# Mixing stage of a two-layer kernel: outputs made one step later, masks last in GpSimd's step, and two small jobs that change engines

## The reference, cut to what matters

```
bc = einsum('bti,oi->bto', value, W_bc)          # per token: 32 heads x (Bz, Bx, Cz, Cx) x 32
bc = bc / (sqrt(sum(bc*bc, -1)) + EPS)
step: z = S*(z - dt*A*s + dt*(Bz x u));  s = s + dt*z + dt*(Bx x u)
      y = Cz.z + Cx.s
y = (y + skip*value) * silu(gate)
out = einsum('bti,oi->bto', y, W_out)
```

## Time and profile before

| | us |
|---|---|
| median of 3 runs (1324.44 to 1331.52) | 1328.13 |
| the profiled execution's own time | 1331.72 |
| its span | 1329.6 |
| TensorE busy, share of the span | 96% |
| VectorE busy | 68% |
| ScalarE busy | 49% |
| GpSimd busy | 44% |

### The profile page before, as it was taken

One profiled execution on the slowest core, in us unless ns is written; L12 is line 12 of the kernel. 1 busy time (PEld: TensorE's weight loads), 2 busy tenths in 40 slices (PEclk: granted clock), 3 DMA queues, 4 the chain that ended last, 5 costly groups with the idle time before them and its releaser, 6 DMA issues. The chain is left out here.

```text
span 1329.6 us, 23001 instructions
## 1 busy us (share of the span) xinstructions
PE 1279.4 (96%) x7802; PEld 705.5 (53%) x7802; DVE 910.6 (68%) x1771; ACT 651.5 (49%) x1564; POOL 588.8 (44%) x939
## 2 busy tenths in 40 slices
PE   7999998999999999998899998999999999999999
PEld 4443334566566566565445454555655556544545
DVE  6999996999999999997301206888787786630100
ACT  3265533566665665664322315665565666531221
POOL 2633323888888988987100002444444453500000
PEclk7989999999999999998899999999999999999999
DMA  3369897656656665664100002000000000000000
GB/s 99 127 264 394 338 393 273 215 191 224 201 201 212 220 203 196 223 213 167 64 0 0 1 0 90 1 1 1 1 1 1 2 1 1 1 0 0 16 0 16
DMA packets 72834, 151.38 MB, mean 114 GB/s; under 512 B 7312, under 2 KB 24336, under 8 KB 69904
## 3 DMA queue, kind: packets, MB, share of 16 engines
q1 hardware_dynamic: 66096, 133.66, 28.5%
q10 hardware_dynamic: 6624, 16.26, 3.2%
HBM read 98.78 MB, written 51.12 MB: 113 GB/s over the span
## 5 line engine op out<-in xcount | busy, mean ns | idle before, releaser
L1869 POOL TENSOR_SCALAR pr<-pr,rs,sg 128x512 f32<-128x512 f32 (+3 forms) x256 | 152.6, 614 | 204.9 <-DVE rs L1774 186.1
L720 PE MATMUL banks<-w_bc,valueT 128*128 128x512 f32 x392 | 185.1, 596 | 3.4 <-ACT ent L593 2.4
L1046 DVE TENSOR_TENSOR pp<-banks,ring 128x1024 f32<-128x1024 f32 x128 | 156.1, 1220 | 12.8 <-DVEq L1083 5.5
L1675 ACT ACTIVATE pr<-banks,nm 128x512 f32<-128x512 f32 (+3 forms) x256 | 132.8, 524 | 20.4 <-DVE nm L1768 17.7
L1663 ACT COPY prT<-banks 128x512 f32<-128x512 f32 (+3 forms) x128 | 54.3, 424 | 112.5 <-PE banks L1544 112.3
L1768 DVE TENSOR_REDUCE nm<-banks 128x2 f32<-128x1024 f32 (+3 forms) x128 | 105.5, 824 | 4.4
L1384 DVE TENSOR_TENSOR x<-x,banks 128x256 f32<-128x256 f32 x16 | 6.7, 421 | 148.3 <-PE banks L1295 148.3
L935 ACT COPY qk<-banks 128x512 f32<-128x512 f32 x128 | 74.8, 585 | 63.0 <-PE banks L834 63.0
L672 POOL TENSOR_TENSOR C<-abL,A 128x128 f32<-128x128 f32 x128 | 53.3, 424 | 104.9 <-DVE banks L347 91.8
L1544 PE MATMUL banks<-ident,pr 128*128 128x128 f32 x640 | 96.9, 281 | 2.1 <-POOL pr L1869 0.7
L1130 POOL TENSOR_SCALAR_AFFINE_SELECT bp<-bp 128x1024 f32<-128x1024 f32 x64 | 73.8, 1152 | 55.9 <-ACT bp L942 55.9
(11 more groups left out here) (254 smaller groups left out, 2499.6 us busy)
## 6 DMA issues: line engine op xcount, KB each, us to landing
ring<-psi SPq DMA_DIRECT2D x126, 512.0 KB, 4.4
psi<-ring SPq DMA_DIRECT2D x10, 2048.0 KB, 7.5
psi<-X SPq DMA_DIRECT2D x5, 2048.0 KB, 7.5
det<-w_bc ACTq DMA_DIRECT2D x16, 512.0 KB, 4.7
ring<-det SPq DMA_DIRECT2D x64, 128.0 KB, 4.7
bcs<-ent ACTq DMA_DIRECT2D x30, 256.0 KB, 6.9
ring<-bcs SPq DMA_DIRECT2D x30, 256.0 KB, 5.0
w_bc<-in_w_bc SPq DMA_DIRECT2D x4, 1024.0 KB, 10.9
```

The costliest lines, as they stand in the source:

```text
L720: mm = pe.matmul(bank, m["valueT"][:, c, t * P:(t + 1) * P], w, start=(c == 0), stop=(c == 1))
L1046: dve.tensor_tensor(pp[:, q % 2].rearrange("p (a c) n -> p a c n", c=2), sc.unsqueeze(2).broadcast_to([P, 4, 2, HN]), rec[:, n % RL, q % 2 ...
L1675: act.activation(pr[:, n % RP, h, 0:w], S[n % 2][:, h, 0:w], ACT.Exp, bias=nm[:, n % 4, h:h + 1], accum_out=sm[:, m % 3, n % 2, h:h + 1]). ...
L1869: pool.tensor_scalar(row, row, rs[:, n // 2 % 2, n % 2, h:h + 1], sg[:, TPB * b + it, hd:hd + 1], ALU.mult, ALU.mult).then_inc(s["scaled"], 1)
```

## The change

What is done:

- On TensorE `outputs` of pair p-1 are made in step p, right behind `scores` of pair p. The loop gets one step more. `turn_state` and `project_out` come one step later, in even steps, behind the first `project`, and write into columns 192 to 447 of the bank YG and not into TP. Their waits on other banks go with them.
- On ScalarE `take` moves ahead of the two `copy_qk`, the spreading of the state and the copy to oc stand between them, and `expand_u` is made here for tiles 2 to 15.
- On VectorE `evacuate` is gone. GpSimd makes it, in odd steps.
- On GpSimd both `combine` come first, then `evacuate`, then `mask(p)`, then the rest. `expand_u` stays there for tiles 0 and 1 only.
- The ring ct is three units deep and not two.

The pieces of the diff stand in the order TensorE, ScalarE, VectorE, GpSimd.

```diff
-    RL, RB, RC, RQ = 3, 3, 2, 4
+    RL, RB, RC, RQ = 3, 3, 3, 4
+    STATE = 2 * N + P
...
             def turn_state(t, f):
-                pe.transpose(TP[:, 0:P], hT[:, f].rearrange("p a n -> p (a n)"), k.ident[:]).then_inc(s["turned"], 1)
+                pe.transpose(YG[:, STATE:STATE + P], hT[:, f].rearrange("p a n -> p (a n)"), k.ident[:]).then_inc(s["turned"], 1)
             def project_out(t):
-                    mm = pe.matmul(TP[:, P:2 * P], yg[:, t % 2, f], w_out[:, f], start=(f == 0), stop=(f == 1))
+                    mm = pe.matmul(YG[:, STATE + P:STATE + 2 * P], yg[:, t % 2, f], w_out[:, f], start=(f == 0), stop=(f == 1))
...
-            for p in range(2 - LEAD, PAIRS + 2):
+            for p in range(2 - LEAD, PAIRS + 3):
                 if 0 <= p < PAIRS:
                     scores(2 * p)
                     scores(2 * p + 1)
+                if 1 <= p <= PAIRS:
+                    outputs(2 * p - 2)
+                    outputs(2 * p - 1)
                 for u in range(2):
                     if 0 <= p + 1 < PAIRS:
                         turn_both(2 * p + 2 + u)
                     if 2 <= p + LEAD < PAIRS:
                         project(2 * (p + LEAD) + u)
-                if 0 <= p < PAIRS:
-                    outputs(2 * p)
-                if p >= 3 and p % 2 == 1:
-                    t, f, j = split(2 * (p - 2))
-                    pe.wait_ge(s["qk"], min(2 * p + 4, UNITS))
-                    if passes_on(t):
-                        turn_state(t, f)
-                    if f == 1:
-                        project_out(t)
-                if 0 <= p < PAIRS:
-                    outputs(2 * p + 1)
+                    if p >= 4 and p % 2 == 0 and u == 0:
+                        t, f, j = split(2 * (p - 4))
+                        pe.wait_ge(s["ygc"], min(p, PAIRS) // 2)
+                        if passes_on(t):
+                            turn_state(t, f)
+                        if f == 1:
+                            project_out(t)
...
+                if 2 <= p <= PAIRS and p % 2 == 0:
+                    take(p // 2 - 1)
                 if 0 <= p + 1 < PAIRS:
                     copy_qk(2 * p + 2)
-                    copy_qk(2 * p + 3)
-                if 2 <= p + LEAD < PAIRS:
-                    square(p + LEAD)
-                if p >= 3 and p % 2 == 1:
-                    t, f, j = split(2 * (p - 2))
+                if p >= 4 and p % 2 == 0:
+                    t, f, j = split(2 * (p - 4))
...
+                if 0 <= p + 1 < PAIRS:
+                    copy_qk(2 * p + 3)
+                if 2 <= p + LEAD < PAIRS:
+                    square(p + LEAD)
+                if p >= 4 and p % 4 == 1 and p // 4 + 1 < TILES:
+                    expand_u(p // 4 + 1)
...
                     if passes_on(t):
                         state(t, f)
-                    evacuate(t, f)
...
+            def evacuate(t, f):
+                tok = slice(t * P, (t + 1) * P)
+                pool.wait_ge(s["ygc"], 2 * t + f + 1)
+                if t >= 2:
+                    pool.wait_ge(s["out"], t - 1)
+                pool.tensor_tensor(yg[:, t % 2, f], ygc[:, f, 2 * N:], m["gateT"][:, f, tok], ALU.mult).then_inc(s["yg_done"], 1)
...
                 if p + 1 < PAIRS:
                     combine(2 * p + 3)
+                if p + 2 < PAIRS:
+                    combine(2 * p + 4)
+                if p >= 3 and p % 2 == 1:
+                    t, f, j = split(2 * (p - 2))
+                    evacuate(t, f)
                 if p >= 0:
                     mask(p)
-                if p + 2 < PAIRS:
-                    combine(2 * p + 4)
                 if p >= 7 and p % 4 == 3:
                     residual(p // 4 - 1)
-                if p >= 4 and p % 4 == 1 and p // 4 + 1 < TILES:
-                    expand_u(p // 4 + 1)
```

More of the change, by code:

```diff
@@ L823, in turn_both @@
                     pe.wait_ge(s["qk"], q)
-                if q >= 10 and q % 4 == 2:
-                    t, f, j = split(q - 7)
-                    if passes_on(t):
-                        pe.wait_ge(s["hz"], 2 * (links(t, f) + 1))
-                    if f == 1:
-                        pe.wait_ge(s["oc"], t + 1)
                 for pair in range(2):
@@ L855, in outputs @@
                         pe.wait_ge(s["ygc"], q // 4)
-                    if carried(t):
-                        pe.wait_ge(s["hz"], 2 * (links(t - 1, f) + 1))
+                    if q >= 8:
+                        ts, fs, js = split(q - 8)
+                        if passes_on(ts):
+                            pe.wait_ge(s["hz"], 2 * (links(ts, fs) + 1))
+                        if fs == 1:
+                            pe.wait_ge(s["oc"], ts + 1)
                 for i in range(4):
@@ L963, in spread_state, with expand_u @@
                     act.copy(dst, src).then_inc(s["hz"], 1)
+            def expand_u(t):
+                act.wait_ge(s["yg"], HG * (t - 1))
+                for f in range(2):
+                    dst = uz[:, t % 2, f].rearrange("p (j e) -> p j e", e=DIAG)[:, :, 0:P].rearrange(
+                        "p j (i e) -> p j i e", i=4)[:, :, :, 0:DH]
+                    act.copy(dst, m["u"][:, t, f * P:(f + 1) * P].rearrange("p (i j d) -> p j i d", i=4, j=4)
+                             ).then_inc(s["uz"], 1)
             def moments(t):
@@ L998, in _ @@
                             act.wait_ge(s["x"], t)
-                        act.copy(oc[:], TP[:, P:2 * P]).then_inc(s["oc"], 1)
-                if 0 <= p < PAIRS and p % 2 == 1:
-                    take(p // 2)
+                        act.copy(oc[:], YG[:, STATE + P:STATE + 2 * P]).then_inc(s["oc"], 1)
+                if 0 <= p + 1 < PAIRS:
[4 more added lines that the diff above has]
+                    expand_u(p // 4 + 1)
                 b, i = divmod(p - 20, 16)
@@ L1067, in state @@
                                   tv[:, :, 1].unsqueeze(1).broadcast_to([P, 2, 2, N]), ALU.add).then_inc(s["hT"], 1)
[L1069 to L1074, removed]
             def invert(b):
@@ L1099, in _ @@
                         state(t, f)
-                    evacuate(t, f)
                 if q % 2 == 0 and q // 2 % 16 == 12 and q // 2 >= 28:
                     invert(q // 32 - 1)
-            evacuate(TILES - 1, 0)
-            evacuate(TILES - 1, 1)
         @block.gpsimd
@@ L1160, in _ @@
                     combine(2 * p + 3)
+                if p + 2 < PAIRS:
[3 more added lines that the diff above has]
+                    evacuate(t, f)
                 if p >= 0:
                     mask(p)
-                if p + 2 < PAIRS:
-                    combine(2 * p + 4)
                 if p >= 7 and p % 4 == 3:
                     residual(p // 4 - 1)
-                if p >= 4 and p % 4 == 1 and p // 4 + 1 < TILES:
-                    expand_u(p // 4 + 1)
                 if p >= 28 and p % 16 >= 12:
                     normalise(TPB * (p // 16 - 1) + p % 16 - 12)
+            evacuate(TILES - 1, 1)
             residual(TILES - 1)
```

6 lines of the change are left out of this document (1 added, 5 removed).

## The result

| | before | changed |
|---|---|---|
| median, us | 1329.89 (6 runs) | 1354.33 (6 runs) |
| ratio, with 95% interval | | 1.0208 (1.0183 to 1.0234) |
| profiled execution, us | 1331.72 | 1359.22 |
| its span | 1329.6 | 1357.5 |
| from the first scores to the transposes of the next stage | 411.1 | 433.8 |

The forecast was 1362 in a range from 1319 to 1398; the change costs 24.4 us where 34 were forecast. The last line of the table is the length of the mixing: the scores start at 230.2 before and at 230.5 now, the transposes of the next stage at 641.3 and at 664.2. The stage grew by 22.7. The profiled execution is 27.9 longer in span, of which 4.9 lie behind the mixing; in all other kernels of this study that part took 688 to 690 us, here 693, and this execution lies 4.9 over its own median, so I read it as a matter of this one execution.

What follows compares the result with a forecast made beforehand. TensorE was taken as a close bound. 24 double steps with `state` (340 us) plus 8 without (100) against 402 gave +38, less 4: +34 on 1331.7, or 1366; 3.6 over the median, so 1362, range 1319 to 1398.

Steps and rivals of the forecast that it cites:

- What bounds the kernel before: Mixing: TensorE, needing some 12.4 of 12.74 us per double step; VectorE slack by what it loses at the lock.
- TensorE's own gain: Mixing, TensorE: 0.33 us of waits and turn lost, a new wait gained; net -0.14 per double step, bounds -0.33 and 0.
- The place of the mask: Mixing, GpSimd against VectorE: combines run when VectorE wants two-input instructions; double step with a state becomes 14.15 us.
- (1): GpSimd's even combine waits for a bp buffer freed by the later outputs, so starts about 1.0 us after product Q.
- (2): VectorE's three state instructions each wait for a combine instruction (1.82, 2.57, 3.26); product Q+1 ends at 4.39, not 3.04.
- (3): GpSimd's mask ends at 4.64 and VectorE's small product waits for it, to 4.68; product Q+2 ends at 7.75.
- (4): Next mask starts just before VectorE's small product, which waits for all of it, to 11.08; product Q+4 ends at 14.15.
- its signs: Small product's mean 0.8 or more, state instructions 0.5 or more, idle time ahead of combines, TensorE waiting, scores every 14.1.
- the record of 4.80 at 617: End of the mixing, VectorE: a one-time state record some 4.6 us too long before goes away, -4 us.
- no change: Whole kernel: TensorE's gain and VectorE's loss cancel, or the new wait eats the gain; 1324 to 1333 us, chance 0.13.
- the faster case: Mixing: VectorE's waits don't grow and TensorE keeps the pace; -8 to -14, about 1317 to 1320 us, chance 0.20.
- Starvation: Mixing, VectorE: state gets in only when GpSimd goes idle; 46 us more, 1408; chance 0.15, wholly or in part.

Runs made afterwards that it cites:

- x2: Kernel before, without VectorE's small 32-column product (weights and small constant missing from the result): 1324.95 us, ratio 0.9977 to before.
- x1: Changed kernel without VectorE's small 32-column product (weights and small constant missing from the result): 1318.46 us, ratio 0.9939 to before.
- x3: Changed kernel with the ring bp four pairs deep and not three: 1343.73 us, ratio 1.0117 to before.
- x10: Changed kernel with one more GpSimd wait: the mask is held in every step until VectorE's small 32-column product has run: 1318.57 us, ratio 0.9929 to before.
- x8: Changed kernel with the gated product (`evacuate`) back on VectorE, behind the state: 1381.52 us, ratio 1.0402 to before.
- x4: Changed kernel with the mask put back between GpSimd's two combines: 1329.74 us, ratio 1.0009 to before.
- x7: Kernel before, with VectorE's small 32-column product moved to GpSimd as two small instructions: 1382.13 us, ratio 1.0410 to before.
- x6: Changed kernel with the small product moved to GpSimd and, in even steps, outputs between the two units' scores on TensorE: 1354.50 us, ratio 1.0192 to before.
- x9: Changed kernel with GpSimd's mask held in even steps only until VectorE's small 32-column product has run: 1327.79 us, ratio 0.9992 to before.

## Why the prediction was right, point by point

*What bounds the kernel before.* Right: TensorE, with VectorE's waits at the port as slack. x2 shows the second half, 2.9 us for 63 instructions whose records hold 36 us; for the first speak TensorE's 39.7 of 40 us.

*TensorE's own gain.* About right, though the differences that show it are small. 0.14 per double step was forecast. In x1, which lacks L1032, the 16 double steps of the second and third sequence take 201.15, and 202.87 in the kernel before: 0.11 each. At the first tiles of the second to fourth sequence the double steps took 11.86 to 12.88 before (mean 12.22) and take 11.92 now, 0.30 less. The new wait for the copy is 0.3 where I had 0.2.

*The place of the mask.* Right, step by step, in the double step shown above, counted from the end of product Q at 401.11:

| step | forecast | measured |
|---|---|---|
| (1) combine(Q) starts | 1.0 | 0.89 |
| (2) L1064, L1068, L1074 end | 1.82, 2.57, 3.26 | 1.69, 2.44, 3.18 |
| (2) product Q+1 ends | 4.39 | 4.31 |
| (3) mask ends, L1032 behind it | 4.64, 4.68 | 4.60, 4.63 |
| (3) product Q+2 ends | 7.75 | 7.70 |
| (4) L1032 behind the mask ends | 11.08 | 11.01 |
| (4) product Q+4 ends | 14.15 | 14.09 |

In the other form of the double step (1) is 1.06, L1064 doesn't wait, product Q+1 ends at 3.85, L1032 ends at 4.86 and product Q+4 at 14.32. The forecast had only the first form, and that both come out alike in length was not foreseen. So one of its signs is not met: L1064 was to rise to 0.5 or more and its mean is 0.405, since 7 of its 16 records are 0.65 and 9 are 0.21 or 0.22. The others are: a mean of 0.816 for L1032 with 35 of 63 records over 1.0, 0.70 and 0.68 for L1068 and L1074, GpSimd's idle time ahead of its combines, TensorE's waits for the product, and scores every 14.1 to 14.3.

x3 shows (1) by taking its cause away, x1 and x10 show (3) and (4), x8 shows the same port with one instruction more, and x4 that without the mask's new place the loss is gone by the medians.

*The sum* is where the forecast was off: +34, measured +24.4, and 22.7 in the stage. Three terms of it were mis-sized. The 8 double steps without a `state` I put at 12.5, TensorE's mean; they lie at the first tile of each sequence, where TensorE has no carried state to multiply, and take 11.9: 8 x 0.6 = 5 too many. The 24 double steps of 14.15 are 22, because the last two states fall behind the last projection, where the double step is not VectorE's: about 2 x 0.7 there (the last of them is 13.5). And I set 32 double steps against 402, which is the length of 63 steps; 32 double steps of 12.74 are 408, so the sum started 6 too high. 34 less these 12 is 22, and the stage grew by 22.7. The 4 that were taken off for the record of 4.80 at 617 came out near: from the scores of pair 60 to the transposes of the next stage it was 30.66 and is 27.42. That this record is the reason is not shown; x1 has a record of 5.42 and takes 26.53 there.

*The range.* 1319 to 1398 also takes in no change and the upper end of the faster case, so that a time within it says little. The inner bounds, 1340 to 1385, hold 1354 as well, and what bears the mechanism out is the table above and the experiments.

*The rivals.* Starvation did not come: the longest L1064 is 0.651, where 4.8 stood before. The faster case, TensorE keeping the pace, did not come by itself, but it is what x10 makes: 1318.6, where the rival had given 1317 to 1320. That the number fits is in part luck: the rival took 0.14 to 0.33 off every double step, and in x10 the double steps of the second and third sequence are as long as before.

*What went unforeseen* was not in the prediction but in the experiments: x7 and x6, both of which moved a hand-over into a queue that was late, or asked for a result earlier than that queue gives it.

## What to carry to other kernels

When two engines share a port, a wait on one of them may be the slot in which the other works, so before taking an idle time away, look what runs in it. A record that is several times as long as its shape explains, and that ends a few hundredths behind another engine's record, was held back by it here each time: compare ends, not durations, and find out by leaving the instruction out whether it is slack or the bound. Where such a lock binds, ordering the two instructions with one more wait can be worth more than moving work: here the same kernel went from 2.1% slower to 0.7% faster with it. And where a variant comes out ahead, look in which part of the stage it does, before you credit its pace.

## What the runs showed of the hardware

An instruction of VectorE with two inputs in SBUF holds its record open while GpSimd's current instruction runs, and ends 0.03 to 0.15 us behind it (0.03 to 0.05 with 32 columns, 0.08 with 64, 0.15 with 128 in the changed kernel), both for a mask of 1.15 and for each of three products of 0.73 to 0.78 in a row; with one input in PSUM (the products, 1.22) or one in SBUF (the reciprocal, 0.353) it runs beside GpSimd at an unchanged length. The profile counts this waiting as busy time: VectorE looks 38 of 40 us busy both where it is the bound and where it is not.

Not every end of a GpSimd instruction lets it in. In x1 and in x2 again one record of the state's first product held on for 5.42 and 5.09 us while GpSimd ran eight and seven instructions without a gap, as the 4.80 in the kernel before, each time in the last steps. In x3 three records of L1032 took 1.75, 1.73 and 1.30: they began under the third instruction of a combine, passed its end by, and waited for the mask too. In x9 one took 1.57, through all three instructions of a combine. In the changed kernel 59 of the 63 ended 0.03 to 0.05 behind an instruction of GpSimd with its next one directly behind, and none was longer than 1.15. What tells these cases apart stays open, and no run was made for it.
